# First norm kept in place over the input, its transposes and queries moved into the turn before

## What is computed

```python
x = layernorm(x + random_feature_attention(x))       # first norm (ln1)
x = layernorm(x + cross_attention(x, ctx))            # ln2, 16 heads, 120 keys
x = layernorm(x + coupling_ffn(x))                    # ln3, 3 cycles of a small gelu network and a rotation
x = layernorm(x + mamba(x))                           # ln4, 512 channels x 16 states, a scan along the tokens
x = layernorm(x + gated_context(x, ctx))              # ln5
x = layernorm(x + mixture_of_experts(x))              # ln6, 8 experts, the best one taken
```

## Time and profile before

| | |
|---|---|
| time, median of three runs | 3096.45 us (3095.3 to 3101.43) |
| profiled execution | 3099.29 us, of which the span from first to last instruction is 3097.5 us |
| PE busy | 2540.1 us, 82% |
| DVE busy | 2495.3 us, 81% |
| ACT busy | 1727.8 us, 56% |
| POOL busy | 1487.4 us, 48% |
| DMA | 45.72 MB, 15 GB/s on average |

### The profile page before, as it was taken

One profiled execution on the slowest core, in us unless ns is written; L12 is line 12 of the kernel. 1 busy time (PEld: TensorE's weight loads), 2 busy tenths in 40 slices (PEclk: granted clock), 3 DMA queues, 4 the chain that ended last, 5 costly groups with the idle time before them and its releaser, 6 DMA issues.

```text
span 3097.5 us, 41602 instructions
## 1 busy us (share of the span) xinstructions
PE 2540.1 (82%) x11020; PEld 1469.9 (47%) x11020; DVE 2495.3 (81%) x4288; ACT 1727.8 (56%) x3062; POOL 1487.4 (48%) x1159
## 2 busy tenths in 40 slices
PE   6896888979888897888988788888888889887556
PEld 3544554544444454445545444554544445454323
DVE  2368888897978889898888978788897888978783
ACT  1457564646657474665646466564656646465620
POOL 1046354554535455563545545354553545456460
PEclk7868888888989989999898899898898989978687
DMA  3000000000000000000000000000000000000000
GB/s 131 10 8 10 14 11 14 17 14 7 10 21 10 14 17 14 7 10 21 10 14 13 18 7 10 21 10 14 13 3 21 10 14 7 7 7 1 14 7 7
DMA packets 16849, 45.72 MB, mean 15 GB/s; under 512 B 2248, under 2 KB 7056, under 8 KB 16400
## 3 DMA queue, kind: packets, MB, share of 16 engines
q1 hardware_dynamic: 16656, 43.96, 4.2%
HBM read 35.57 MB, written 8.39 MB: 14 GB/s over the span
## 4 chain that ended last, share of the span: by engine, by line
PE 47%; DVE 28%; issue 14%; ACT 7%; DVEq 2%; POOL 1%; ACTq 0%; DMA 0%; SPq 0%; POOLq 0%
PE bank L535 45%; DVE h_ring L1087 14%; DVE x L1199 3%; DVE ln_stats L387 2%; DVE smax L991 1%; POOL ysum L1671 1%; ACT a_ring L1479 1%; DVE x L405 1%; DVE xpad L1093 1%; PE bank L413 1%; DVE soft L1066 1%; ACT L1485 1%; ACT L1339 1%; DVE ln_mv L391 1%; ACT spare L1420 1%
## 5 line engine op out<-in xcount | busy, mean ns | idle before, releaser
L1671 POOL TENSOR_TENSOR ysum<-ysum,h_ring 128x512 f32<-128x512 f32 x896 | 1155.2, 1289 | 633.3 <-DVE h_ring L1087 571.3
L1087 DVE TENSOR_TENSOR_SCAN h_ring<-a_ring,bank 128x512 f32<-128x512 f32 x1024 | 1172.7, 1200 | 27.2 <-ACT bank L1474 16.2
L1479 ACT ACTIVATE a_ring<-soft,decay 128x510 f32<-128x510 f32 x1024 | 675.7, 717 | 198.4 <-DVE h_ring L1087 198.0
L535 PE MATMUL bank<-w_expert_w,x45T 128*128 128x512 f32 x1024 | 541.1, 675 | 199.0 <-DVE x L1199 191.4
L535 PEld LDWEIGHTS bank<-w_expert_w,x45T 128*128 128x128 f32 x1024 | 213.2, 216 | 490.9 <-DVE x L1199 253.5
L1658 POOL TENSOR_TENSOR soft<-xc,soft 128x512 f32<-128x512 f32 x64 | 81.0, 1276 | 655.2 <-ACT soft L1457 655.2
L535 PE MATMUL bank<-x3T,w_winT 128*128 128x512 f32 x512 | 291.0, 704 | 39.7 <-ACT x3T L419 31.4
L991 DVE TENSOR_REDUCE smax<-bank 128x4 f32<-128x480 f32 x256 | 156.4, 652 | 143.1 <-PE bank L535 143.1
L535 PE MATMUL bank<-qT,kmask 32*120 32x256 f32 x1024 | 207.2, 497 | 50.2 <-ACT spare L1386 40.6
L535 PE MATMUL bank<-spare,w_cn_w 128*128 128x256 f32 x768 | 217.7, 408 | 37.0 <-ACT spare L1416 22.4
L1199 DVE SCALAR_TENSOR_TENSOR x<-bank,weight,x 128x256 f32<-128x256 f32 x512 | 212.5, 474 | 40.4 <-PE bank L535 40.4
(11 more groups left out here) (149 smaller groups left out, 3890.2 us busy)
## 6 DMA issues: line engine op xcount, KB each, us to landing
x0T<-in_xT SPq DMA_DIRECT2D x16, 512.0 KB, 3.3
x<-in_x SPq DMA_DIRECT2D x16, 512.0 KB, 4.3
out<-x SPq DMA_DIRECT2D x16, 512.0 KB, 3.0
ctxT<-in_ctxT SPq DMA_DIRECT2D x16, 240.0 KB, 2.5
ctxTb<-in_ctxT SPq DMA_DIRECT2D x16, 240.0 KB, 2.7
ctxb<-in_ctx SPq DMA_DIRECT2D x16, 240.0 KB, 3.0
w_expert_w<-in_expert_w SPq DMA_DIRECT2D x1, 2048.0 KB
w_winT<-in_winT SPq DMA_DIRECT2D x1, 1024.0 KB
```

The costliest lines, as they stand in the source:

```text
L535: return pe.matmul(o, l, r, start=start, stop=stop)
L1087: scanned.then(v.tensor_tensor_scan(h_ring[:, k % HRING, :], a_ring[:, k % RING, :, :].rearrange("p b s -> p (b s)"), xc2, 0.0, ALU.mult, ...
L1479: a.activation(a_ring[:, k % RING, :, 1:S], delta[:, c, :].rearrange("p (b s) -> p b s", b=NB)[:, :, 1:S], ACT.Exp, scale=decay[:, k:k + 1 ...
L1671: p.tensor_tensor(out=total, in0=first, in1=h_ring[:, k % HRING, :], op=ALU.add)\
```

## The change

The first norm writes its result over the input tile `x0` (where its sum stands already) and its transposed result over `feats`. It shares nothing any more with the second norm. `add_bias` reads it from `x0` and writes to `x12`. The rest follows in the order of work:

- DVE: `ln1_sum(nxt)` ahead of scans 48 and 49, the apply behind them.
- ACT: the first norm's rstd between decays 57 and 58, the copies of its transposes behind the last decay, the query copies behind the sixth norm's rstd and the last rotation; the third norm's rstd comes last.
- PE: the transposes between the last four steps of the experts, two and two, into the banks of the first projection; the queries behind the last cycle into banks 1 and 0; two chunks of `mamba_out`, `rotate_back`, one more chunk. In the next turn's head the first scores come ahead of three input projections, the second ahead of the fourth.
- POOL: `add_bias` waits for the first norm's apply and the third norm's sum; `norms` also waits for the queries.
- SP: the input tile is free once `add_bias` and the transposes are done.

```diff
-        n1, n2, n3 = Norm("ln1", x12, x12T, x0), Norm("ln2", x12, x12T), Norm("ln3", x3, x3T, sum3)
+        n1, n2, n3 = Norm("ln1", x0, feats), Norm("ln2", x12, x12T), Norm("ln3", x3, x3T, sum3)
...
-        QUERY = [bank[2], bank[0]]
-        TURN1 = [bank[0], bank[1]]
+        QUERY = [bank[1], bank[0]]
+        TURN1 = OUT1
...
             def x_free(g):
-                sp.wait_ge(n1.x_ready.sem, n1.x_ready.at(g, NT))
+                sp.wait_ge(x1b_ready.sem, x1b_ready.at(g, 1))
+                sp.sem_inc(held.sem, 1)
+                sp.wait_ge(n1.turned.sem, n1.turned.at(g, DC))
...
-            def queries(g):
+            def queries(g, f):
+                if f is not None:
+                    pe.wait_ge(gate_ready.sem, gate_ready.at(f, CYC))
                 pe.wait_ge(n1.xT_ready.sem, n1.xT_ready.at(g, DC))
...
-                if f is not None:
-                    norm_turn(pe, n1, f, TURN1)
                 if m is not None:
                     norm_turn(pe, n3, m, TURN)
-                    mamba_in(m, b, 0, 2)
-                if f is not None:
-                    queries(f)
-                if m is not None:
-                    mamba_in(m, b, 2, 3)
                 if f is not None:
                     scores(f, 0, 1)
                 if m is not None:
+                    mamba_in(m, b, 0, 3)
+                if f is not None:
+                    scores(f, 1, 2)
+                if m is not None:
                     mamba_in(m, b, 3, 4)
-                if f is not None:
-                    scores(f, 1, 2)
...
-                    experts(b, 12, 16)
+                    experts(b, 12, 14)
+                if nxt is not None:
+                    norm_turn(pe, n1, nxt, TURN1)
+                if b is not None:
+                    experts(b, 14, 16)
                 if f is not None:
                     cycle(f, 2 * NB)
-                if m is not None:
-                    mamba_out(m, 0, IC - 1)
+                if nxt is not None:
+                    queries(nxt, f)
+                if m is not None:
+                    mamba_out(m, 0, 2)
                 if f is not None:
                     rotate_back(f, 0)
+                if m is not None:
+                    mamba_out(m, 2, IC - 1)
...
                     combine(b, 10, 12)
+                if nxt is not None:
+                    ln1_sum(nxt)
                 states(m, 52)
                 if nxt is not None:
-                    ln1_sum(nxt)
-                states(m, 54)
+                    norm_apply(v, n1, nxt)
...
-                if nxt is not None:
-                    norm_apply(v, n1, nxt)
...
-            def queries(g):
+            def queries(g, f):
+                if f is not None:
+                    a.wait_ge(z_ready.sem, z_ready.at(f, 2 * CYC))
...
+                decays(m, 58)
+                if nxt is not None:
+                    norm_rstd(a, n1, nxt)
                 decays(m, STEPS)
+                if nxt is not None:
+                    norm_copy(a, n1, nxt, TURN1)
                 if f is not None:
                     cycle(f, 2 * NB)
                     nat()
+                if b is not None:
+                    norm_rstd(a, n6, b)
                 if nxt is not None:
-                    norm_rstd(a, n1, nxt)
+                    queries(nxt, f)
                 if f is not None:
                     norm_rstd(a, n3, f)
-                if b is not None:
-                    norm_rstd(a, n6, b)
...
+                    p.wait_ge(q_psum.sem, q_psum.at(g, 0))
...
-            def add_bias(g):
-                p.wait_ge(n1.turned.sem, n1.turned.at(g, DC))
+            def add_bias(g, m):
+                p.wait_ge(n1.x_ready.sem, n1.x_ready.at(g, NT))
+                if m is not None:
+                    p.wait_ge(n3.sum_ready.sem, n3.sum_ready.at(m, 2))
```

More of the change, by code:

```diff
@@ L835, in turn @@
                 if m is not None:
-                    mamba_in(m, b, 3, 4)
+                    mamba_in(m, b, 0, 3)
                 if f is not None:
                     scores(f, 1, 2)
+                if m is not None:
+                    mamba_in(m, b, 3, 4)
                 if b is not None:
@@ L926, in _ @@
             first_project(0)
+            norm_turn(pe, n1, 0, TURN1)
+            queries(0, None)
             turn(0, None, None, 1)
@@ L1509, in turn_ @@
             def turn_(f, m, b, nxt):
-                if f is not None:
-                    norm_copy(a, n1, f, TURN1)
                 if m is not None:
@@ L1517, in turn_ @@
                 if m is not None:
-                    mamba_in(m, 0, 2)
-                if f is not None:
-                    queries(f)
-                if m is not None:
-                    mamba_in(m, 2, IC)
+                    mamba_in(m, 0, IC)
                 if b is not None:
@@ L1613, in _ @@
             norm_rstd(a, n1, 0)
+            norm_copy(a, n1, 0, TURN1)
+            queries(0, None)
             turn_(0, None, None, 1)
@@ L1681, in turn_ @@
                 if f is not None:
-                    add_bias(f)
+                    add_bias(f, m)
                 if nxt is not None:
```

## The result

The changed kernel takes 3194.22 us (median of four runs, 3192.27 to 3195.61), the kernel before 3095.88 us beside it (3092.76 to 3101.43). The ratio is 1.0311, 95% interval 1.0292 to 1.0329. The sign was as predicted. The size was not: 34 us were predicted, 98 measured, and the range ended at 3150. The kernel before was timed again beside every later run; its medians lie between 3095.88 and 3099.74, so differences between runs made at different times are good to some 4 us.

The account below looks back on a forecast made before the run. No engine's total decides: DVE bounds the tail, a relay of engines the head. Twelve loop ends (24.1), two straight ends (6.4) and turn 0 (3.2) give +33.7 on the profiled 3097.5, adjusted to 3130 us; range 3103 to 3150.

Parts of the forecast that it names:

- (1): Tail, DVE before scan 48: a new wait of 2.0 us for ACT's Square behind the first norm's rstd; bounds 1.4 to 2.3.
- (2): Tail, DVE behind scan 49: the first norm's apply adds 2.3 us, 1.28 of pitch plus 1.03 beside POOL's add.
- (3): Tail, PE: the first norm's transposes, some 1.1 us, fall into the 5.00 us wait ahead of the last experts, costing nothing.
- (4): Tail, PE: queries behind the last cycle fit ahead of the Mamba residual with 0.4 us to spare; at half clock, 3.2 cost.
- (5): Tail, PE: Mamba output between the two rotate-backs adds 0.2 us; the third norm's statistics end 4.55 later in all.
- (6): Head, ACT: jump wait stays 2.5 us, x3T copies end 4.2 after the third norm's statistics, first convolution at 8.6.
- (7): Head, PE: idles 4.3 us ahead of the second scores, fourth projection behind them; the head gives back 2.5 us.
- (8): Head, PE clock: low clock behind the new wait costs 0 to 1.4 us a turn, set against 1.2 saved: zero.
- (9): Edges outside the loop: two straight turn ends at +3.2 us each, turn 0 at +3.2; the input load costs nothing.
- low clock at the new wait: Rival: PE's low clock there in every turn and nothing saved at the head, 20 us more, 3150; chance 0.2.

## Why the prediction was wrong, step by step

In the turn shown, A is 1237.51 and T 1277.63 (end of the statistics of the third norm).

(1) The wait for the Square: 2.0 predicted, 1.89 measured. Right. (2) The apply: 2.3 and 2.31. Right; the value was taken from the earlier trace rows rather than from the pitch, and that was the right choice. (3) The transposes lie in PE's wait ahead of the last experts and cost nothing:

```profile
1245.21 0.33 PE L413 MATMUL bank<-w_ident,x 128*128 128x128 f32 x1 [3.90 <-DVE x L405]
1246.49 1.98 PE L413 MATMUL bank<-w_ident,x 128*128 128x128 f32 x7 [0.95 <-DVE x L405]
1248.31 4.48 PE L537 MATMUL bank<-w_expert_w,x45T 128*128 128x512 f32 x8
```

The experts start at A+10.8, predicted A+10.9. (4) The queries end ahead of the residual, which waits for DVE's combine alone, and stands at A+29.5 (predicted A+29.2):

```profile
1261.56 3.69 PE L537 MATMUL bank<-feats,w_wq 128*128 128x512 f32 x8 [0.72 <-ACT gate L1440]
1267.03 1.98 PE L537 MATMUL bank<-x,w_ident 128*128 128x512 f32 x4 [1.77 <-DVE x L1208]
```

(5) T should move by 4.55. Measured to the third norm's sum, from 30.22 + 2.24 to 36.86, it is 4.4; to the end of its statistics, from A+35.6 to A+40.1, it is 4.5. The whole tail was right.

(6) *The first failed step: ACT's wait at the jump.* It was taken over as 2.5 us. It was 4.84, so the x3T copies ended at T+6.5 instead of T+4.2. The trace of before had a hint that I cited and did not use: in the earlier trace rows ACT waits 2.51 ahead of the first three copies and 0.64 more ahead of the fourth, which starts 4.7 us behind the end of the last activation ahead of the jump. A fixed price of a jump has no second part. The changed program has six more ACT instructions ahead of the loop, which put its start at the worst place found. Cost of this step: 12 × 2.3 = 28 us by the rows, and 26 measured where seven increments lengthen the wait of the kernel before from 2.51 to 4.68. The 42 of the run with 16 increments are more than that step: they take away the whole wait (the copies end at T+3.5, earlier than predicted) and 21 of them come from the stretch between the last maximum and the choice of the expert.

(7) PE's wait ahead of the second scores: 4.3 predicted, 4.42 measured. Right, and so was the order behind it.

(8) *The second failed step: the clock at a net of zero.* PE was at 1.2 GHz from the first scores on in all 12 turns, where the forecast had hoped to save even the 1.2 us a turn that six turns pay before. Behind the wait of 4.42 it was there again; the term of 0 to 1.4 forgot the scores. The projection costs 1.77 more, the scores 0.89. The head does not give 2.5 us back: the second convolution stands at T+24.3, predicted T+17.85. Of these 6.5, 2.3 are the jump, 1.6 the clock in the first projections and 2.6 the clock behind the wait. The Trainium skill, "TensorE: Matmul & The Clock Gate", section "HAM oscillation — how this bites in real kernels", says that a long wait for data takes PE back to the low clock and that the next matmuls start cold. The trace agrees at this wait: 0.52 in the window behind the 4.42 us.

Over a loop turn this is less than it looks. Before, the heads were on average 1.1 us longer than the one that the prediction started from, the stretches between second convolution and first norm's sum gave 1.1 more back than the 2.24 of the moved sum, and the tail cost 0.5 less against the mean turn. So a turn is 3.9 longer than predicted (5.90 against 2.0), 47 us in twelve.

(9) The edges: 9.6 predicted, about 25 measured. s of turn 0 comes 8.6 later, where 6.9 was predicted for T, and the 3.7 that the following head was to give back don't come: s of turn 1 is 6.9 later again against before, s of turn 2 another 8, s of turn 15 2.8 less, and the end behind it 4.7 more. The heads of these straight turn ends are at the low clock as the others are (11.6 and 11.9 between the convolutions, 9.6 before). The input load cost nothing: the only waits for a DMA in the trace are three at the program's start, for its constants.

The rival "low clock at the new wait" (3150) was the nearer one, but gave the forecast only 20 us more. With its 20 and the 28 of the jump the sum is 3178, against 3194 measured; the rest is clock that it too left out, 0.9 a turn for the scores behind the wait and 1.6 for the first projections, less what other stretches give back.

The placement explains a miss of the prediction, but not why the changed kernel is slower. Padded by 16 in both, the change costs 3152.70 − 3050.27 = 102 us, and with the loop at 312 in both 68. In the kernel before the shorter wait of 2.5 us cost as much (48 us) as the longer one did in the changed kernel (42), where PE's low clock hides part of it. What makes the mean turn 5.9 us longer is the tail with 4.1 more, for which the head gives nothing back: up to the second convolution it is 2.9 longer itself, and 1.1 come back between it and the tail.

## What to carry to other kernels

When two versions of a kernel with a hardware loop differ by a per cent, look at the first instructions behind the jump on each engine: a wait put down to "issue" there can belong to the placement of the loop and not to the edit. A few idle instructions ahead of the loop tell the two apart, and so does the page's count of "instruction" packets (171 against 111 here). Compare the two versions at equal placement. Emptying PE's list ahead of a wait is not free: here a wait of 4.42 us was followed by the low clock, one of 2.80 too in the two heads outside the loop, and one of 2.70 in the loop was not, so price everything behind a lengthened wait at the low clock too, and put work ahead of the wait rather than behind it. And edits priced one by one on a relay of engines don't add up.

## What the runs showed of the hardware

ACT's first instructions behind a taken jump wait for nothing of their own, for 2.5 to 3.6, or for 4.5 to 5.0 us, by the place of the loop in ACT's program alone; for the kernel before that is 3050 to 3134 us. The longest come just ahead of an edge (312, 568), the free ones behind it, and the pattern repeats at a distance of 254 to 263 instructions. With a wait there are five more packets of code for each jump. The Trainium skill, "Runtime: NRT & Kernel Launch", section "Instruction fetch mechanics", says that an engine's code comes in blocks of 256 instructions, that most engines hold two, that fetching ahead is sequential, and that a taken branch to a block that isn't held has to fetch it first. The runs with 263 and 271 increments agree with it. That the wait of 4.7 is two fetches in a row fits the packets at 4.6 and 7.2 us behind s. That a jump from 694 on pays because the block after next is already being loaded over the one with the target fits the table, and was not tried on its own.

What PE, DVE and POOL pay at their jumps was not tried; the counts were varied on ACT only.
